# Loading the first expert's weights from ScalarE's queue during routing, in a graph network with a mixture of experts

## The reference

```python
logits = xt @ Wr + br
probs = softmax(logits)
top_p, top_idx = top_k(probs, 2)
weights = top_p / top_p.sum(-1, keepdims=True)
xn = (xt - mean) * rsqrt(var + 1e-5)
xe = xn[None] * ln_g[:, None, :] + ln_b[:, None, :]          # per expert
h = gelu(einsum('end,edh->enh', xe, W1) + b1[:, None, :])    # W1: 8 x 256 x 1024
y = einsum('enh,ehd->end', h, W2) + b2[:, None, :]           # W2: 8 x 1024 x 256
out = sum over the two chosen experts of weight * y
```

## Time and profile before

| what | us |
|---|---|
| median of three runs | 3188.27 (3187.75 to 3189.39) |
| profiled execution, its own time | 3191.06 |
| its span, first to last instruction | 3189.4 |
| edge tables and node phase | about 245 |
| edge phase | about 1984 |
| routing | about 214 |
| experts | about 670 |
| combination | about 76 |

### The profile page before, as it was taken

The page is one execution under the profiler, slowest core; times in us unless marked ns, Lnnn a source line. Parts: engine busy times, 40 slices in busy tenths (PEclk is TensorE's granted clock), DMA queues, the critical chain, the costliest instruction groups (busy, mean ns, idle before and its releaser), DMA issues. The chain is left out here.

```text
span 3189.4 us, 46614 instructions
## 1 busy us (share of the span) xinstructions
PE 2071.1 (65%) x12432; PEld 1745.7 (55%) x12433; DVE 1937.4 (61%) x5386; ACT 861.3 (27%) x2271; POOL 1775.1 (56%) x1829
## 2 busy tenths in 40 slices
PE   3775666666666666666666666665342999999990
PEld 2444444444444444444444444444332999999980
DVE  6545666666666666666666666666783665656655
ACT  1222222222221112222222221111441555555540
POOL 1006777777777777777777777775475222212110
PEclk7997887878888888888878787777555999999995
DMA  1333444444444444444444444443444222212117
GB/s 44 112 110 101 109 108 108 109 108 108 109 108 108 109 108 108 109 108 108 109 108 108 109 108 108 109 108 83 136 138 137 66 79 64 86 56 73 41 43 241
DMA packets 192452, 327.35 MB, mean 103 GB/s; under 512 B 70287, under 2 KB 124542, under 8 KB 192428
## 3 DMA queue, kind: packets, MB, share of 16 engines
q0 software_dynamic: 98560, 256.53, 29.4%
q1 hardware_dynamic: 74328, 51.16, 5.7%
q10 hardware_dynamic: 19540, 19.40, 1.9%
HBM read 278.03 MB, written 47.99 MB: 102 GB/s over the span
## 5 line engine op out<-in xcount | busy, mean ns | idle before, releaser
L620 POOL DMA_INDIRECT rows<-proj_table,idx x1568 | 1486.3, 948 | 711.1 <-issue 418.2
L665 PE MATMUL banks<-weighed,onehot 128*128 128x264 f32 x3136 | 1082.8, 504 | 740.3 <-DVE weighed L736 739.5
L665 PEld LDWEIGHTS banks<-weighed,onehot 128*128 128x128 f32 x3136 | 735.5, 246 | 913.9 <-issue 767.6
L840 ACT ACTIVATE banks<-score,neg_bound 128x32 f32<-128x32 f32 x392 | 114.1, 291 | 1572.5 <-DVE score L729 1572.5
L726 DVE TENSOR_TENSOR raw_score<-rows,target 128x32 f32<-128x32 f32 x392 | 75.3, 192 | 717.4 <-DMA rows<-proj_table,idx 715.2
L736 DVE TENSOR_TENSOR weighed<-rows,banks 128x1024 f32<-128x1024 f32 x392 | 473.6, 1208 | 0.0
L1456 POOL DMA_INDIRECT results_by_token<-yrow,goes_to x104 | 108.9, 1047 | 478.6 <-DVE yrow L1404 350.4
L1343 ACT ACTIVATE hid<-banks,params 128x256 f32<-128x256 f32 x416 | 198.1, 478 | 267.7 <-PE banks L1299 261.1
L702 DVE TENSOR_TENSOR onehot<-banks,key_tab 128x512 f32<-128x512 f32 x397 | 270.1, 681 | 0.0
L1392 DVE TENSOR_TENSOR hidl<-hid,hidh 128x256 fp32r<-128x256 f32 x416 | 169.8, 424 | 149.7 <-ACT hidh L1337 149.5
L1299 PE MATMUL banks<-f_xth,w1h 128*128 128x256 f32 x832 | 236.4, 284 | 28.0 <-ACT hid L1343 14.5
(11 more groups left out here) (235 smaller groups left out, 2871.5 us busy)
## 6 DMA issues: line engine op xcount, KB each, us to landing
rows<-proj_table,idx POOLq DMA_INDIRECT x1568
w_raw<-in_L_ffn_W_dram POOLq DMA_DIRECT2D x16, 1024.0 KB, 6.3
xrow<-tokens_by_expert SPq DMA_DIRECT2D x106, 128.5 KB, 2.1
c_y<-results_by_token SPq DMA_DIRECT2D x10, 1120.0 KB
proj_table<-trow ACTq DMA_DIRECT2D x50, 128.9 KB
xin<-in_x_dram SPq DMA_DIRECT2D x50, 125.0 KB
skip_rows<-srow ACTq DMA_DIRECT2D x50, 125.0 KB
r_skin<-skip_rows SPq DMA_DIRECT2D x10, 625.0 KB
```

What stands on the lines that cost most here:

```text
L620: nc.gpsimd.indirect_dma_start(rows[k][:, i, :], None, table, bass.IndirectOffsetOnAxis(ap=idx[pair][:, col:col + 1], axis=0)).then_inc(ga ...
L665: mm = nc.tensor.matmul(acc_bank[u // 2 % 2][:, 0:ROW], onehot[u][:, i, :], weighed[:, k * SET + i, :], start=(u % 2 == 0 and i == 0), sto ...
```

## The change

The three raw buffers are allocated before the routing phase, with a semaphore `first_loaded` for the first expert's load. ScalarE issues the six transfers of expert 0 in routing, between `exponential(0)` and `deviations(0)`, and waits for them at the end of its list in routing. In the expert phase GpSimd no longer does `load(0)`, and ScalarE and VectorE don't wait before the splits of expert 0. `load(1)` to `load(7)` stay on GpSimd's queue as they were; the counts they are waited for by are one load lower.

```diff
+        m.update(w1_raw=sb("w1_raw", [P, KD, HID]), w2_raw=sb("w2_raw", [P, JH, D]), params_raw=sb("params_raw", [P, PARAMS]),
+                 first_loaded=ctx.enter_context(nc.semaphore("first_loaded")),
+                 expert_inputs=(W1, W2, ln_g, ln_b, b1, b2))
         route_phase(nc, m, bank, x, skip_rows, xg)
...
+def weight_loads(m, e):
+
+    W1, W2, ln_g, ln_b, b1, b2 = (w[bass.ds(e, 1)] for w in m["expert_inputs"])
+    params = m["params_raw"]
+    return ((m["w1_raw"][:], W1.rearrange("o (k p) h -> p (o k) h", p=P)),
+            (m["w2_raw"][:], W2.rearrange("o (j p) d -> p (o j) d", p=P)),
+            (params[:, GAIN:GAIN + KD], ln_g.rearrange("o (k p) -> p (o k)", p=P)),
+            (params[:, SHIFT:SHIFT + KD], ln_b.rearrange("o (k p) -> p (o k)", p=P)),
+            (params[:, B1:B1 + JH], b1.rearrange("o (j p) -> p (o j)", p=P)),
+            (params[:, B2:B2 + D], b2.to_broadcast([P, D])))
...
             exponential(0)
+            with nc.allow_non_contiguous_dma(reason="small rows of parameters, once an expert"):
+                for to, of_expert in weight_loads(m, 0):
+                    act.dma_start(to, of_expert).then_inc(m["first_loaded"], 16)
             deviations(0)
...
+            act.wait_ge(m["first_loaded"], 16 * 6)
             act.wait_ge(count_ready, 1)
             nc.scalar.activation(m["gaps"][:], m["gaps"][:], ACT.Exp).then_inc(weight_exp, 1)
...
             def split_high(e, s):
-                act.wait_ge(raw_loaded, 16 * W_LOADS * (e + 1))
+                if not isinstance(e, int) or e > 0:
+                    act.wait_ge(raw_loaded, 16 * W_LOADS * e)
...
             def split_low(e, s):
-                dve.wait_ge(raw_loaded, 16 * W_LOADS * (e + 1))
+                if not isinstance(e, int) or e > 0:
+                    dve.wait_ge(raw_loaded, 16 * W_LOADS * e)
...
-            load(0)
             load(1)
```

More of the change, by code:

```diff
@@ L65 @@
 CAP = -(-(N + TOK) // TOK) * TOK
+GAIN, SHIFT, B1, B2 = 0, KD, 2 * KD, 2 * KD + JH
+PARAMS = 2 * KD + JH + D
 FILL = TOK
@@ L1220, in sems @@
             return [sem(f"{name}{k}") for k in range(n)]
-        w1_raw, w2_raw = sb("w1_raw", [P, KD, HID]), sb("w2_raw", [P, JH, D])
-        params_raw, params = sb("params_raw", [P, 2 * KD + JH + D]), sb("params", [P, 2, 2 * KD + JH + D])
+        w1_raw, w2_raw, params_raw = m["w1_raw"], m["w2_raw"], m["params_raw"]
+        params = sb("params", [P, 2, 2 * KD + JH + D])
         w1h, w1l = sb("w1h", [P, 2, KD, HID], F32R), sb("w1l", [P, 2, KD, HID], F32R)
         w2h, w2l = sb("w2h", [P, 2, JH, D], F32R), sb("w2l", [P, 2, JH, D], F32R)
-        GAIN, SHIFT, B1, B2 = 0, KD, 2 * KD, 2 * KD + JH
         xrow = sb("xrow", [P, HALF, XROW])
@@ L1424, in load @@
             def load(e):
[L1426 to L1432, removed]
-                with nc.allow_non_contiguous_dma(reason="small rows of parameters, once an expert"):
[L1434 to L1441, removed]
+                pool.wait_ge(w_low, 3 * e)
+                pool.wait_ge(w_high, 2 * e)
+                with nc.allow_non_contiguous_dma(reason="small rows of parameters, once an expert"):
+                    for to, of in weight_loads(m, e):
                         pool.dma_start(to, of).then_inc(raw_loaded, 16)
```

## The result

The changed kernel takes 3183.57 us (median of 20 runs) against 3188.55 for the kernel before in the same sessions (20 runs): ratio 0.9986, 95% interval 0.9979 to 0.9992, so 4.5 us faster (2.6 to 6.7). The ratio is that of the means; the medians lie 5.0 apart. The forecast was 5.7. The profiled execution has a span of 3183.1 against 3189.4; 3.06 of these 6.3 us were won before routing began, in phases that the change doesn't touch, and are the spread between executions. From here on moments of routing are therefore counted from the start of VectorE's first reciprocal, which opens routing in every run.

A forecast was written before the change was run, and what follows sets the result against it. Bound at the seam by a chain of weight loads, splits and Gelu, no engine over 65% busy. Gain 10.2 less a 4.5 stall: 3188.27 - 5.7 = 3182.6 us; 8-in-10 range 3177.5 to 3193.0.

The forecast's parts named there:

- late tiles: Routing, chunk 1: weights share DMA engines with SyncE's tiles, `xin` 1 lands 7.0 us later, the logits come 4.5 later.
- The seam: From routing to the expert phase: load 0 goes from the chain of waits, TensorE restarts earlier; gain 10.2 us.
- The cover for `normalize(0)`: Head of expert phase: transposed rows may delay normalising by 4.06 us, but TensorE waits for a Gelu anyway; cover over 2.
- Six issues on ScalarE: Routing, before the first square root: six issues of 0.51 us, 3.0 in all, hidden in 6.2 free.
- If ScalarE's queue is as deep and its own, nothing is held: ScalarE's issues in routing: 184 pieces on each of 16 engines, against 250 for two transfers on SyncE's queue.
- The tiles: Routing, chunk 1: `xin` 1 lands at 2261.95 instead of 2254.95, delaying VectorE's logits by 4.5 us.
- `skin` 1: Routing, chunk 1: this tile would be late by 1 to 3 us, inside the same wait as `xin` 1.
- No stall: Rival, routing: SyncE's stream goes first or engines take both streams without loss; 3178.1 us, chance 0.13.
- ScalarE held behind SyncE's full queue: Rival, routing: ScalarE's issues wait for SyncE's at a shared generator, root 9.6 to 14.8 late; 3187.7 to 3192.9 us, chance 0.36.
- In line, slower: Rival, routing: one line serves both queues' transfers strictly in order, root up to 26.0 late; up to 3204.1 us, chance 0.10.

The follow-up runs named there:

- the small ones first: Changed kernel with ScalarE issuing the four small transfers of expert 0 before its two weights; 3183.58 us, a single run.
- only the weights on ScalarE: Changed kernel with ScalarE issuing only the two weights, GpSimd the four small transfers at the head of routing; 3182.36 against 3187.19 us, ratio 0.9985.
- the parts alone: Changed kernel with each of SyncE's routing tiles loaded in two parts, of 112 and 13 partitions; 3182.12 against 3187.19 us, ratio 0.9982.

## Why the prediction was right, point by point

**The total: right, in part by luck.** The forecast added 4.5 for late tiles to a gain of 10.2. What the changed kernel paid in routing was 5.6, and it paid nearly all of it for ScalarE's own issues, a term that the forecast had put at nothing. Had the two costs added up, 5.8 and the 5.1 seen with the small ones first, nothing would have been left of the gain.

**The seam: right.** 10.2 forecast, 9.9 measured, and by the way described: ScalarE's first split 1.40 after its table load, load 1 right behind the splits, the restart 23.2 after the phase began (22.9 forecast). The cover for `normalize(0)` wasn't needed: without load 0 beside them the rows were turned by 2451.65, before the splits ended at 2453.60.

**Six issues on ScalarE: wrong, and this is the step that failed.** "Six issues of 0.51 are hidden" read a price from transfers that met an empty queue. They took 13.3 from Relu's start on, where ScalarE had 7.6 free (the 6.2 and Relu's own 1.36), and the root came 5.8 late. The sentence "If ScalarE's queue is as deep and its own, nothing is held" counted 184 pieces against 250 on each engine; the third issue was held with 96 pieces or fewer on each (1536 in all, if evenly spread). So depth on SyncE's queue, read from pieces of 1 KB, didn't carry over.

**The tiles: right in kind, and masked.** The forecast stall was 4.5; where ScalarE was free the logits came 5.1 late (small first, with a wait of 7.59 for `xin` 1). In the changed kernel the late root had used up that time, and 1.09 of waiting was left. The two costs lie side by side and the larger counts, 5.8 here. That is why the total came out at -4.3 by the profile for -5.7 forecast, although a cost had been overlooked. `skin` 1 was later than the 1 to 3 forecast: SyncE's next issue, which ends when that tile is through, took 12.69 and ended some 6.8 later than before.

**The rivals.** *No stall*: out, by the runs with only the weights on ScalarE and with the small ones first, where VectorE waited 4.18 and 7.59. *ScalarE held behind SyncE's full queue*: the effect came (a late root, by 5.8 rather than 9.6 to 14.8), and with issues of several us, which by the prediction were its signs, but its mechanism is not the one described. ScalarE's two big issues went through in 0.44 and 0.48 while SyncE's fourth was held for 5.80 (2234.18 to 2239.98), and the hold appears without SyncE's stream. The lock of the generator that the Trainium skill describes ("Perfetto Trace Analysis", "DMA Instruction — HWDGE") did not keep ScalarE out while SyncE's instruction stood waiting for room; no run here shows such a long lock. *In line, slower*: did not come.

**What stays open** is what a queue counts. With the weights first, the third to sixth issue wait (4.69, 1.67, 1.46, 4.42), with the small ones first hardly. With the weights first the six took 8.7 without SyncE's tiles, 13.3 beside tiles on a third of the engines, 14.7 beside tiles on all, 13.4 and 21.0 on SyncE's own queue, and 4.5 on GpSimd's. Pieces on each engine (250 on SyncE's, held under 100 on ScalarE's), pieces in all (some 1700 on SyncE's in two parts, held from 1250 on without) and bytes (2 MB pass on ScalarE's, 1.25 MB fill SyncE's) each contradict one run. The order of sizes and the issuing engine matter, and more isn't shown.

## What to carry to other kernels

Price an issue by the state of its queue, not by the fastest issue in the trace: large transfers ahead of small ones can hold the issuing engine for about as long as their data flows (8.7 to 14.7 us here on ScalarE), so put small ones first, or issue from an engine that has nothing to do until they land. A load that is moved out of a wait meets the transfers of its new place: ask which of those is needed next, and look there for idle DMA time before looking for an idle engine. When two delays end at one wait, only the larger shows, so removing one may give nothing until the other is gone too (the gain stayed at 5.1 with the parts alone and at 3.6, a single run, with the order alone, and was 15.6 with both).

## What the runs showed of the hardware

A tile of 125 partitions moves at 112 GB/s with 0.34 of the DMA engines busy; in parts of 112 and 13 the tiles flowed at 251 GB/s with all of them (the kernel before in two parts), and the first two waits fell from 3.5 and 4.3 us to 0.7 and 1.1. The Trainium skill, "DMA: Bandwidth & Descriptors", section "Why a DMA increments its semaphore by 16 and not by 1", says that a transfer runs on the largest number of engines up to 16 that divides the slowest dimension of both its sides. By that rule 125 partitions use five engines and 112 use sixteen. The share of 0.34, 5.4 of 16 engines, agrees with the first; the share of 1.08 agrees with the second as far as it can, as a value over 1 says that all were busy but is no count. The kernel before had 4.4 us to gain there, apart from any weights.

The order of six transfers on ScalarE's queue, same bytes and same place, changed the time that they held it from 13.3 to 4.3 us, and from 14.7 to 6.3 beside tiles in two parts. The same six, weights first, held GpSimd for only 4.5.

Where ScalarE's and SyncE's transfers met on SyncE's five engines, SyncE's share fell from 33.6% to 15.6% of all engines' time, about half.
